# Attention inside a two-layer network: order of projections, f32r transposition of maxima, and who loads and places what

## The chip, the core and the metric

The kernel runs on one core of a Trainium2 chip. The metric is the device time in microseconds of one execution. The core has TensorE (matmul), VectorE, ScalarE, GpSimd and SyncE, which here does nothing but issue DMAs; each works through its own instructions in order, and semaphores tie them together.

## What is computed

The reference is a network of two layers on an x of 2 x 1024 tokens with 256 features. Four branches are added to x one after another:

```
x = x + L0_attn(L0_cond(x))        # causal attention, 16 heads of 16
x = x + L0_ffn(L0_cond2(x))        # mixture of MLPs, then a filter in frequency
x = x + L1_attn(L1_cond(x))        # chosen expert, then a recurrent layer
x = x + L1_ffn(L1_cond2(x))        # layer norm, attention, layer norm, mixture of experts
```

Only the two attentions and the stages just ahead of them matter here. An attention is

```
q, k, v = h @ Wq, h @ Wk, h @ Wv                  # (2, 1024, 16 heads, 16)
scores  = q @ k^T, -inf above the diagonal
out     = softmax(scores / 4) @ v @ Wo (+ bo)
```

## The kernel before

The stages (`prepare`, `attention` "a0", ..., `gated_weight`, `layer_norm`, `attention` "a1", ...) stand one behind another, each a block with one program per engine and a barrier at its end. `first_branches` and `last_branch` call them.

An attention works in eight groups (NG): 2 batches times 4 sets of 4 heads. A group has the following steps.

- `qk`: two projections (one per half h of the 1024 tokens) of queries and keys, in f32 (`qk_projection`, L487). ScalarE rounds each to f32r (`upper`, L602), VectorE subtracts what was rounded off (`lower`, L637); both parts go to the tile `comp`. ScalarE does so for a new group only when the DMAs that read `comp` for the group before have landed.
- SyncE copies rows of `comp` by DMA into the layout that the products need: `place_keys` (L413, 6 DMAs, into `kx`, a ring of three) and `place_queries` (L426, 12 DMAs for each half, into `qx`, a ring of two).
- `v`: two projections of the values (L496), copied by VectorE.
- `first`: 48 f32r products of queries by keys in blocks (L512), used only for the maximum of each row, which VectorE takes (`maximum`, L654). There are three PSUM banks for them. The 17th (MAX0 = 16 are ahead of it) is the first that needs the second half of the queries.
- `max`: the negated row maxima, split into two parts, are transposed by matmul with a negated identity (`maxima`, L520), copied by VectorE and placed by 4 DMAs of SyncE (`place_maxima`, L433) as extra rows of `qx`.
- `scores` (L536): 48 products again, transposed and with the maximum subtracted, in 12 steps (STEPS) of 4 heads; ScalarE takes the exponential (L615), GpSimd cuts the diagonal blocks (L466), `values` (L552) multiplies by v.
- `sums` (L561) and `spread` (L571): reciprocals of the sums, multiplied in by VectorE. After the last group, `out` (L584) is the output projection.

All of it is software-pipelined by hand. `before_turns` lists what comes ahead of the first turn: both projections of group 0, its v, its 48 first-pass products, and among them the projections of group 1. `turn(n)` then interleaves, step by step, the scores and values of group n, the first-pass products of group n + 1 (FIRSTS_AFTER says how many after each of the 48 score products), and one small job after each step (SMALL). A pair (name, 2, h) in SMALL is for group n + 2. The resulting list ORDER is walked by every engine, and each picks its own entries. All small jobs share one PSUM bank, so each waits until the one before has been read. The entries `k_slots` and `q_slots` are SyncE's DMAs: keys and the first half of the queries right after the second projection, the second half at the start of the next turn.

In the opening SyncE loads the weights (L400, four DMAs of 256 KB) with the mask (L402) behind the first; VectorE clears `qx` (L632) and waits for the mask ahead of everything else; ScalarE writes rows of ones into `kx` (L605) after its second `upper`. The constants, among them the identity and the negated identity, are loaded in `prepare` (L98).

The order ahead of the first turn and the small jobs, in the code:

```python
FIRSTS_AFTER = ((1, 1, 0, 2), (2, 1, 1, 1), (1, 0, 2, 1), (0, 3, 0, 0),
                (0, 3, 0, 0), (1, 1, 2, 0), (1, 1, 0, 2), (1, 2, 1, 0),
                (1, 1, 1, 1), (1, 2, 0, 1), (2, 0, 0, 2), (1, 3, 0, 1))
SMALL = (("max", 0, 1), ("sums", -1, 1), ("v", 1, 0), ("spread", -1, 1), ("v", 1, 1), ("max", 1, 0),
         ("qk", 2, 0), ("qk", 2, 1), ("sums", 0, 0), None, None, ("spread", 0, 0))
```

## Time and profile before

| | us |
|---|---|
| median of 3 runs | 2849.01 (2847.25 to 2849.82) |
| profiled execution | 2844.19, its span 2842.5 |
| mean granted clock of TensorE | 0.908 |
| first attention: start, first turn, eighth turn | 36.2, 97.3, 417.5 |
| second attention: start, first turn, eighth turn | 1772.8, 1833.7, 2155.6 |

Times in the trace are from the start of the span. TensorE has two clock levels, 1.2 and 2.4 GHz; the granted clock of a stretch is given as a share of the upper one. The lines of matmuls merge instructions of one form that follow one another; their ends are modelled, and they overlap a little. An f32 product shows as two instructions, an f32r product as one. "SPq" is SyncE's queue of DMA issues: its times are those of the issue, not of the transfer.

### The profile page before, as it was taken

Reading aid. Unit: us, or ns where it says so; the run is one execution under the profiler, and the core shown is the slowest. Engines: PE = TensorE matmul, PEld = TensorE weight load, DVE = VectorE, ACT = ScalarE, POOL = GpSimd, SP = SyncE. Lnnn points to the kernel's source line nnn. Section 1 sums busy time; section 2 is a strip of 40 time slices with the busy share of each in tenths; the row PEclk is TensorE's granted clock in tenths of the full one; section 3 lists DMA queues with packets and bytes.
Section 4 is the critical chain, followed back from the end, with each engine's and each line's share of the span. In section 5 each row is a group of like instructions: output and inputs, shape, how many; then the busy total and the mean of one; then the engine's idle time right before and its main releaser. Section 6 shows DMA issues by size and latency. Waiting matters only on the chain. (4 is left out here: it accounts for less than half of the span.)

```text
span 2842.5 us, 33896 instructions
## 1 busy us (share of the span) xinstructions
PE 2370.3 (83%) x11792; PEld 1605.7 (56%) x11792; DVE 1700.3 (60%) x3614; ACT 845.7 (30%) x1605; POOL 387.5 (14%) x274
## 2 busy tenths in 40 slices
PE   6999997799999775666565656799999679999998
PEld 3565653688887543333333332455655458888786
DVE  3766662444443367999999994566663335555544
ACT  2344452222222234111211112254544222222222
POOL 0011110522220300111000110001010121111110
PEclk9899999899999898888788778799999789999999
DMA  4111110311100110000000000211110021111110
GB/s 136 40 30 41 29 32 1 119 45 44 44 15 0 45 65 8 8 8 8 15 0 15 0 0 7 61 29 42 35 35 9 1 76 38 37 37 37 37 37 30
DMA packets 34114, 92.14 MB, mean 32 GB/s; under 512 B 12088, under 2 KB 13112, under 8 KB 30008
## 3 DMA queue, kind: packets, MB, share of 16 engines
q1 hardware_dynamic: 33984, 90.49, 10.5%
q8 instruction: 72, 1.18, 0.2%
q14 instruction: 58, 0.48, 0.1%
HBM read 62.59 MB, written 2.16 MB: 23 GB/s over the span
## 5 line engine op out<-in xcount | busy, mean ns | idle before, releaser
L654 DVE CUSTOM_DVE_ANT_0 a_junk<-pair,a_mask 128x512 f32<-128x512 f32 (+3 forms) x768 | 391.0, 551 | 219.5 <-PE pair L512 218.6
L615 ACT ACTIVATE a_prob<-pair 128x512 f32<-128x512 f32 (+3 forms) x768 | 326.8, 494 | 383.3 <-PE pair L536 380.4
L512 PE MATMUL pair<-a_kx,a_qx 96*128 96x512 f32 (+3 forms) x768 | 261.3, 397 | 56.4 <-DMA a_qx<-a_comp 44.9
L536 PE MATMUL pair<-a_qx,a_kx 98*128 98x512 f32 (+3 forms) x768 | 272.1, 401 | 5.6 <-ACT a_prob L615 5.4
L906 DVE TENSOR_TENSOR mx_h<-pair,mx_g 128x512 f32<-128x512 f32 x128 | 88.5, 692 | 264.3 <-PE pair L725 253.8
L723 PE MATMUL pair<-mx_x_hi,mx_w_lo 128*128 128x512 f32 x512 | 201.4, 393 | 23.7 <-POOL mx_w_lo L787 21.1
L723 PE MATMUL pair<-m_x_hi,m_w_lo 128*128 128x512 f32 x448 | 178.3, 398 | 49.4 <-POOL m_w_lo L787 47.4
L512 PEld LDWEIGHTS pair<-a_kx,a_qx 96*128 96x128 f32 x768 | 153.4, 209 | 108.6 <-issue 60.2
L1247 PE MATMUL pair<-h_stream,r_w_kz 128*128 128x512 f32 x192 | 103.6, 693 | 118.8 <-DVE r_region L1653 113.3
L724 PE MATMUL pair<-mx_x_hi,mx_w_hi 128*128 128x512 f32 x512 | 200.3, 391 | 0.0
L725 PE MATMUL pair<-mx_x_lo,mx_w_hi 128*128 128x512 f32 x512 | 200.2, 391 | 0.0
L906 DVE TENSOR_TENSOR m_h<-pair,m_g 128x512 f32<-128x512 f32 x96 | 66.4, 691 | 220.4 <-PE pair L725 219.3
L536 PEld LDWEIGHTS pair<-a_qx,a_kx 98*128 98x128 f32 x768 | 143.4, 194 | 87.3 <-ACT a_prob L615 45.1
L859 ACT ACTIVATE mx_g<-pair 128x512 f32<-128x512 f32 x128 | 76.6, 598 | 385.6 <-PE pair L725 385.6
L466 POOL TENSOR_SCALAR_AFFINE_SELECT a_prob<-a_prob 128x512 f32<-128x512 f32 x128 | 81.5, 637 | 778.0 <-ACT a_prob L615 778.0
L724 PE MATMUL pair<-m_x_hi,m_w_hi 128*128 128x512 f32 x448 | 177.3, 396 | 0.0
L725 PE MATMUL pair<-m_x_lo,m_w_hi 128*128 128x512 f32 x448 | 177.0, 395 | 0.0
L552 PE MATMUL pair<-a_prob,a_v 128*32 128x512 f32 (+3 forms) x1536 | 164.3, 500 | 1.3 <-POOL a_prob L466 1.2
L1291 PE MATMUL pair<-r_hq,r_spread 128*128 128x256 f32 x320 | 85.9, 435 | 84.3 <-DVE r_region L1782 71.5
L859 ACT ACTIVATE m_g<-pair 128x512 f32<-128x512 f32 x96 | 57.4, 598 | 294.7 <-PE pair L725 294.7
L1247 PEld LDWEIGHTS pair<-h_stream,r_w_kz 128*128 128x128 f32 x192 | 41.0, 224 | 172.8 <-DVE r_region L1653 116.5
L1667 DVE TENSOR_TENSOR r_region<-r_region 128x1536 f32<-128x1536 f32 (+7 forms) x160 | 130.0, 854 | 2.7
(250 smaller groups left out, 4447.4 us busy)
## 6 DMA issues: line engine op xcount, KB each, us to landing
m_raw<-in_L_cond_experts SPq DMA_DIRECT2D x18, 1024.0 KB, 4.9
a_kx<-a_comp SPq DMA_DIRECT2D x96, 128.0 KB, 2.4
a_qx<-a_comp SPq DMA_DIRECT2D x384, 32.0 KB, 1.9
mx_raw<-in_L_ffn_experts SPq DMA_DIRECT2D x24, 512.0 KB, 5.4
mx_wt<-expert_weights SPq DMA_DIRECT2D x8, 1024.0 KB, 4.7
r_w_ring<-in_r_q_w SPq DMA_DIRECT2D x8, 512.0 KB
m_raw<-in_L_cond_experts SPq DMA_DIRECT2D x6, 512.0 KB, 3.6
x_stream<-in_x SPq DMA_DIRECT2D x1, 2048.0 KB, 10.1
```

Source lines behind the costliest of these rows:

```text
L512: nc.tensor.matmul(first_bank[t % FR][:, 0:c1 - c0], qx[0:PRODUCT, m % 2, a, i * P:(i + 1) * P], kx[0:PRODUCT, m % 3, a // 2, c0:c1], star ...
L536: nc.tensor.matmul(score_bank[t % SR][:, q0:TT], kx[0:ROWS, n % 3, a // 2, j * P:(j + 1) * P], qx[0:ROWS, n % 2, a, h * TT + q0:(h + 1) * ...
L552: last = nc.tensor.matmul(value_bank[r, q0:TT], v_sb[:, n % 2, j, r], prob[:, i % RING, a, q0:TT], start=j == 0, stop=j == 4 * h + 3)
L615: nc.scalar.activation(prob[:, i % RING, a, q0:TT], score_bank[t % SR][:, q0:TT], ACT.Exp, scale=SCALE).then_inc(s["b_exp"], 1)
L654: nc.vector.tensor_tensor_reduce(out=junk[:, t % 2, 0:cols], in0=first_bank[t % FR][:, 0:cols], in1=mask[:, m0:m0 + cols], scale=1.0, scal ...
L723: nc.tensor.matmul(out, w_lo, x_hi, start=first, stop=False)
L724: nc.tensor.matmul(out, w_hi, x_hi, start=False, stop=False)
L725: return nc.tensor.matmul(out, w_hi, x_lo, start=False, stop=last)
L859: nc.scalar.activation(g_sb[:, n % 2, :], c.quad[2 * (n % 2)], func).then_inc(q["act"], 1)
L906: nc.vector.tensor_tensor(h_sb[:, n % 2, :], c.quad[2 * (n % 2) + 1], g_sb[:, n % 2, :], ALU.mult).then_inc(q["prod"], 1)
L1247: last = nc.tensor.matmul(bank, w_kz[:, k, part * DI + m * P:part * DI + (m + 1) * P], seq(c.h, b)[:, k, half(h)], start=k == 0, stop=k == ...
L1667: did(tt(pr[:, i, :, :, :], right[:, 3 * i:3 * i + 2, :].unsqueeze(1).broadcast_to([P, 3, 2, n]), left.rearrange("p (j q) n -> p q j n", j ...
```

## The change

It has five parts.

1. In each turn the two projections of queries and keys stand after steps 3 and 4 (before: 6 and 7), the two of v after 6 and 7 (before: 2 and 4), and `spread` of the group before after step 2 (before: 3). The first-pass products are distributed anew over the steps.
2. In the opening the projections of group 1 come later: after the 25th and the 29th first-pass product (before: after the 6th and the 10th).
3. The transposition of the maxima uses both operands as f32r. The negated identity is no longer loaded: ScalarE computes it from the identity at the end of `prepare`.
4. The first half of group 0's queries is placed by 12 DMAs that ScalarE issues; SyncE doesn't issue them any more. ScalarE's rows of ones come after them.
5. The weights of queries, keys and values are loaded in the stage ahead of each attention (`prepare`, `gated_weight`) into a tile that both stages share. The mask is then the first load of the attention itself.

```diff
@@ prepare
-                for dst, src in ((c.ident, "ident"), (c.neg_ident, "neg_ident"), (c.mean_ones, "mean_ones"),
+                for dst, src in ((c.ident, "ident"), (c.mean_ones, "mean_ones"),
                                  (c.sum_pick, "sum_pick")):
                     sp.dma_start(dst[:, :], A[src]).then_inc(s["tables"], 16)
-                sp.wait_ge(s["tables"], 4 * 16)
+                load_qkv(c, A, "L0_qkv", sp)
+                sp.wait_ge(s["tables"], 3 * 16)
...
+                act.wait_ge(s["tables"], 3 * 16)
+                nc.scalar.activation(c.neg_ident[:, :], c.ident[:, :], ACT.Copy, scale=-1.0).then_inc(s["out_ev"], 1)
@@ orders
-FIRSTS_AFTER = ((1, 1, 0, 2), (2, 1, 1, 1), (1, 0, 2, 1), (0, 3, 0, 0),
-                (0, 3, 0, 0), (1, 1, 2, 0), (1, 1, 0, 2), (1, 2, 1, 0),
-                (1, 1, 1, 1), (1, 2, 0, 1), (2, 0, 0, 2), (1, 3, 0, 1))
+FIRSTS_AFTER = ((2, 0, 0, 2), (2, 0, 1, 1), (2, 2, 0, 1), (1, 0, 2, 1),
+                (1, 0, 3, 0), (1, 0, 3, 0), (2, 0, 2, 0), (1, 2, 0, 1),
+                (2, 1, 0, 2), (2, 0, 1, 0), (1, 1, 2, 0), (1, 2, 0, 0))
-SMALL = (("max", 0, 1), ("sums", -1, 1), ("v", 1, 0), ("spread", -1, 1), ("v", 1, 1), ("max", 1, 0),
-         ("qk", 2, 0), ("qk", 2, 1), ("sums", 0, 0), None, None, ("spread", 0, 0))
+SMALL = (("max", 0, 1), ("sums", -1, 1), ("spread", -1, 1), ("qk", 2, 0), ("qk", 2, 1), ("max", 1, 0),
+         ("v", 1, 0), ("v", 1, 1), ("sums", 0, 0), None, None, ("spread", 0, 0))
@@ before_turns
-    firsts(0, 6)
-    shared("qk", 1, 0)
-    firsts(6, 10)
-    shared("qk", 1, 1)
-    firsts(10, MAX0)
+    firsts(0, MAX0)
...
-    firsts(MAX0 + 6, NF)
+    firsts(MAX0 + 6, MAX0 + 9)
+    for h in range(HALF):
+        order.append(("qk", 1, h))
+        firsts(MAX0 + 9 + 4 * h, MAX0 + 13 + 4 * h)
+        order.extend(finished("qk", 1, h))
+    firsts(MAX0 + 17, NF)
@@ attention
+def load_qkv(c, A, w_qkv, sp):
+    for g in range(GROUPS):
+        sp.dma_start(c.w_qkv[:, g, :, :, :], A[w_qkv][:, g, :, :, :]).then_inc(c.qkv_in, 16)
...
-                for g in range(GROUPS):
-                    sp.dma_start(w[:, g, :, :, :], A[w_qkv][:, g, :, :, :]).then_inc(s["w_one" if g == 0 else "w_rest"], 16)
-                    if g == 0:
-                        sp.dma_start(mask[:, :], A["causal"]).then_inc(s["mask"], 16)
+                sp.dma_start(mask[:, :], A["causal"]).then_inc(s["mask"], 16)
...
                 def place_queries(m, h):
+                    if (m, h) == (0, 0):
+                        return
...
-                        last = nc.tensor.matmul(bank[0:2 * GH, i * P:(i + 1) * P], mx[:, 4 * h + i, :, :].bitcast(F32).rearrange("p a x -> p (a x)"),
+                        last = nc.tensor.matmul(bank[0:2 * GH, i * P:(i + 1) * P], mx[:, 4 * h + i, :, :].rearrange("p a x -> p (a x)"),
                                                 c.neg_ident[:, :], start=True, stop=True)
...
+                def place_first_queries(m, h):
+                    if (m, h) != (0, 0):
+                        return
+                    act.wait_ge(s["zero0"], GH)
+                    act.wait_ge(s["used"], used("qk", 0, 0))
+                    for a in range(GH):
+                        rows = slice(a * HD, a * HD + HD)
+                        for part, low in enumerate((0, 0, 1)):
+                            r0 = part * 32 + a % 2 * HD
+                            act.dma_start(qx[r0:r0 + HD, 0, a, half(0)].bitcast(F32), comp[rows, low, half(0)].bitcast(F32))\
+                                .then_inc(s["q_in0"], 16)
```

## Rows read from the trace of the kernel before

**Rows 1.** The page, busy time of TensorE: us (share of the span) xinstructions.

```profile
PE 2370.3 (83%) x11792; PEld 1605.7 (56%) x11792; DVE 1700.3 (60%) x3614; ACT 845.7 (30%) x1605; POOL 387.5 (14%) x274
```

**Rows 2.** Stretches: from:to, us, busy us of each engine, granted clock, DMA.

```profile
61.70:97.30 35.60, 29.96 (x64) 16.16 (x65) 25.00 (x98) 1.19 (x2) 0.00 (x0) 0.60 0.23 53
139.90:188.50 48.60, 46.17 (x332) 28.94 (x328) 29.78 (x112) 22.50 (x52) 5.09 (x8) 0.93 0.14 33
188.50:234.10 45.60, 43.20 (x333) 27.22 (x329) 29.70 (x112) 22.14 (x52) 5.09 (x8) 1.00 0.16 37
139.90:417.50 277.60, 263.13 (x1965) 166.00 (x1961) 177.10 (x666) 132.48 (x310) 30.56 (x48) 0.97 0.14 34
1876.80:2155.60 278.80, 264.28 (x1964) 166.46 (x1960) 177.28 (x664) 132.82 (x310) 30.57 (x48) 0.96 0.15 34
```

**Rows 3.** Waits, whole span: who waited for whom, us in total, times, longest.

```profile
PE pair L512 <- DMA a_qx<-a_comp: 44.9, 14, 8.2
```

**Rows 4.** Timeline of SyncE's issues at the end of a turn: start, us, instruction.

```profile
177.81 4.48 SPq L413 DMA_DIRECT2D a_kx<-a_comp  x6
182.39 15.08 SPq L426 DMA_DIRECT2D a_qx<-a_comp  x24
```

**Rows 5.** Timeline of TensorE: end of turn 1, then turn 2 from 188.5.

```profile
185.36 0.22 PE L536 MATMUL pair<-a_qx,a_kx 98*128 98x128 f32 x1
185.42 1.13 PE L512 MATMUL pair<-a_kx,a_qx 96*128 96x512 f32 x3
...
191.39 0.30 PE L512 MATMUL pair<-a_kx,a_qx 96*128 96x128 f32 x1 [2.35 <-DMA a_qx<-a_comp]
193.44 1.04 PE L520 MATMUL pair<-neg_ident,a_mx 128*8 128x128 f32 x8
200.00 2.05 PE L496 MATMUL pair<-a_w,h_stream 128*128 128x128 f32 x16
201.81 0.42 PE L536 MATMUL pair<-a_qx,a_kx 98*128 98x128 f32 x2
202.06 0.74 PE L512 MATMUL pair<-a_kx,a_qx 96*128 96x256 f32 x3
203.36 1.06 PE L571 MATMUL pair<-ident,a_o_rcp 128*32 128x128 f32 x32
```

**Rows 6.** The page, DMA issues: engine, count, KB each, us from issue to landing.

```profile
a_qx<-a_comp SPq DMA_DIRECT2D x384, 32.0 KB, 1.9
m_raw<-in_L_cond_experts SPq DMA_DIRECT2D x6, 512.0 KB, 3.6
a_mask<-in_causal SPq DMA_DIRECT2D x2, 512.0 KB, 5.0
```

**Rows 7.** Timeline, first attention's opening up to its first product.

```profile
39.69 0.91 DVE L632 MEMSET a_qx<- 128x1024 f32 x1 [0.16 <-issue]
40.28 3.68 PE L487 MATMUL pair<-h_stream,a_w 128*128 128x512 f32 x4 [5.09 <-DMA a_w<-in_L_qkv]
45.45 1.98 PE L487 MATMUL pair<-h_stream,a_w 128*128 128x512 f32 x4 [1.49 <-DVE a_comp L637]
48.10 0.69 DVE L637 TENSOR_TENSOR a_comp<-pair,a_comp 128x512 fp32r<-128x512 f32 x1 [2.71 <-ACT a_comp L602]
52.73 15.06 SPq L426 DMA_DIRECT2D a_qx<-a_comp  x24
61.71 2.35 PE L512 MATMUL pair<-a_kx,a_qx 96*128 96x128 f32 x6 [8.25 <-DMA a_qx<-a_comp]
```

**Rows 8.** Timeline, the same opening between its first product and turn 0.

```profile
69.90 0.69 DVE L637 TENSOR_TENSOR a_comp<-pair,a_comp 128x512 fp32r<-128x512 f32 x1 [5.25 <-ACT a_comp L602]
75.53 0.69 DVE L637 TENSOR_TENSOR a_comp<-pair,a_comp 128x512 fp32r<-128x512 f32 x1 [3.28 <-ACT a_comp L602]
80.04 7.79 SPq L426 DMA_DIRECT2D a_qx<-a_comp  x12
97.73 0.31 PE L512 MATMUL pair<-a_kx,a_qx 96*128 96x128 f32 x1
```

More of the change, by code:

```diff
@@ L330, with attention @@
 BANK_OF = {e: n for n, e in enumerate(e for e in ORDER if e[0] in SHARED)}
-def attention(c, A, tag, w_qkv, w_out, b_out, dest):
+def load_qkv(c, A, w_qkv, sp):
+    for g in range(GROUPS):
+        sp.dma_start(c.w_qkv[:, g, :, :, :], A[w_qkv][:, g, :, :, :]).then_inc(c.qkv_in, 16)
+def attention(c, A, tag, w_out, b_out, dest):
     nc = c.nc
     s = {n: c.sem(f"{tag}_{n}") for n in (
-        "mask", "w_one", "w_rest", "proj", "hi", "k_in", "q_in0", "q_in1", "m_in0", "m_in1", "used", "vp", "a_mm",
+        "mask", "proj", "hi", "k_in", "q_in0", "q_in1", "m_in0", "m_in1", "used", "vp", "a_mm",
         "a_max", "m_hi", "m_lo", "t_mm", "b_mm", "b_exp", "b_cut", "pv", "o_sum", "o_cp", "o_spread", "zero0", "zero1", "ones", "ow", "om")}
@@ L416, in place_queries @@
                 def place_queries(m, h):
+                    if (m, h) == (0, 0):
+                        return
                     sp.wait_ge(s["used"], used("qk", m, h))
-                    if m < 2 and h == 0:
+                    if m < 2:
                         sp.wait_ge(s[f"zero{m}"], GH)
@@ L481, in qk_projection @@
                     if h == 0 and m == 0:
-                        pe.wait_ge(s["w_one"], 16)
-                    if h == 0 and m == 1:
-                        pe.wait_ge(s["w_rest"], (GROUPS - 1) * 16)
+                        pe.wait_ge(c.qkv_in, GROUPS * 16)
                     bank = take("qk", m, h)
@@ L602, in upper @@
                     nc.scalar.activation(comp[:, 0, half(h)], bank_of("qk", m, h), ACT.Copy).then_inc(s["hi"], 1)
-                    if m == 0 and h:
-                        for x in range(3):
-                            nc.scalar.activation(kx[PRODUCT:ROWS, x, :, :].rearrange("p q t -> p (q t)"),
-                                                 c.ident[PRODUCT:ROWS, 0:1].broadcast_to([2, PAIRS * T]), ACT.Copy, bias=1.0)\
-                                .then_inc(s["ones"], 1)
+                def place_first_queries(m, h):
[9 more added lines that the diff above has]
+                                .then_inc(s["q_in0"], 16)
+                    for x in range(3):
+                        nc.scalar.activation(kx[PRODUCT:ROWS, x, :, :].rearrange("p q t -> p (q t)"),
+                                             c.ident[PRODUCT:ROWS, 0:1].broadcast_to([2, PAIRS * T]), ACT.Copy, bias=1.0)\
+                            .then_inc(s["ones"], 1)
                 def probabilities(n, i, a):
@@ L1830, in _ @@
                 sp.dma_start(bias[:, :], A["L1_cond2_bias"]).then_inc(loaded, 16)
+                load_qkv(c, A, "L1_qkv", sp)
             @block.tensor
@@ L2068, in first_branches @@
         freq_mat = c.sb("freq_mat", [P, KD, D], ctx=ctx)
-        prepare(c, A, freq_mat)
-        attention(c, A, "a0", "L0_qkv", "L0_wo", "zero_bias", c.x)
+        with ExitStack() as w_ctx:
+            c.w_qkv = c.sb("w_qkv_0", [P, GROUPS, 2, KD, P], ctx=w_ctx)
+            c.qkv_in = c.sem("qkv_in_0")
+            prepare(c, A, freq_mat)
+            attention(c, A, "a0", "L0_wo", "zero_bias", c.x)
         two_of_eight(c, A)
@@ L2077, in last_branch @@
         v = c.sb("branch", [P, KD, N], ctx=ctx)
-        gated_weight(c, A, v)
-        layer_norm(c, A, "n1", v, c.h, "L1_ffn_ln1")
-        attention(c, A, "a1", "L1_qkv", "L1_wo", "L1_bo", v)
+        with ExitStack() as w_ctx:
+            c.w_qkv = c.sb("w_qkv_1", [P, GROUPS, 2, KD, P], ctx=w_ctx)
+            c.qkv_in = c.sem("qkv_in_1")
+            gated_weight(c, A, v)
+            layer_norm(c, A, "n1", v, c.h, "L1_ffn_ln1")
+            attention(c, A, "a1", "L1_wo", "L1_bo", v)
         layer_norm(c, A, "n2", v, c.h, "L1_ffn_ln2")
@@ L2134, in _constants @@
     return {
-        "ident": ident, "neg_ident": -ident, "mean_ones": np.full((P, P), 1.0 / D, f), "sum_pick": pick,
+        "ident": ident, "mean_ones": np.full((P, P), 1.0 / D, f), "sum_pick": pick,
         "causal": causal,
```

6 lines of the change are left out of this document (3 added, 3 removed).

## The prediction

> **What bounds the kernel now.** The share of busy time comes first: TensorE works 83% of the span and is the engine that sets the time in most stages [rows 1]. The chain of waits ends in the last mixture of experts, which the change doesn't touch. The stages run one after another with barriers between them, so what the two attention stages lose or gain is lost or gained in full. Those are the stages to read. The table of stretches, cut at each turn's first score matmul, shows a turn of 45.6 us in which TensorE has 43.20 us of work, VectorE 29.7 and ScalarE 22.1 (the third line of [rows 2]): inside a turn TensorE is the bound, and every matmul taken off it counts. Its missing 2.4 us are the second thing to see. The table of waits has TensorE's line 512 (the first-pass products) waiting for a DMA of queries 14 times, 44.9 us in all [rows 3]. Two of these are the openings, 8.25 us in the first attention [rows 7] and as good as the same in the second, since 8.2 is the longest. The other 12 (one in each turn 1 to 6 of both attentions) hold 44.9 - 2 x 8.2 = 28.5 us, 2.4 each. The timeline shows the place: one score matmul after the turn begins, TensorE sits 2.35 us [rows 5]. SyncE's timeline shows the cause: keys and queries of a group are issued from 177.81 on, some 0.63 us apiece, 6 of keys and 12 of queries, so the twelfth leaves at about 190 and lands 1.9 us later [rows 4, 6]. The projection that releases them comes at the sixth and seventh step, too late by those 2.4 us. The third thing is TensorE's clock: the turn that begins at 139.9 has the same work and the same wait as the one at 188.5, but takes 48.6 us at a mean clock of 0.93 [rows 2]. Half speed (1.2 GHz) shows up right behind the wait.
>
> **Part 1, projections moved from steps 6 and 7 to steps 3 and 4.** The matmuls are the same; they trade places with those of v. Place the landing: the projections end some 13 us sooner in the turn, and 18 DMAs take 11.3 + 1.9 = 13.2 us. So the queries are there 10 us before the turn's end instead of 2.4 us behind it: all 12 waits go, **28.5 us**. What is late next? Queued on SyncE behind them are the maxima's four DMAs (2.5 us), which aren't wanted before the next turn. The second half of the queries, issued at the start of a turn, is now wanted sooner, since the seventeenth first-pass product stands in step 3 and not in step 4. In the turn at 188.5, step 3 begins at 201.81, 13.3 us in [rows 5]. Off that go the wait (2.35), the shorter transposition (0.65, below) and v's 1.8 us, and spread's 1.0 comes in: 9.5 us, and the product stands about 0.9 behind that, at 10.4. Twelve issues and a landing are 12 x 0.63 + 1.9 = 9.5 us after the start. It holds by 0.9 us, and it is the narrowest cover of the change. ScalarE's rounding of the projection waits for the same DMAs, but from step 4 on, some 3 us later. VectorE has 12 us of slack in a turn; the new distribution of first-pass products puts three in a row where three banks are to be had. I take 0 for that, with -3 to +8 us over 14 turns as bounds.
>
> **The clock.** Over turns 1 to 6 it is 0.97 of 277.6 us and 0.96 of 278.8 us [rows 2]: 8.3 and 11.2 us of full clock not granted. How much of that the time feels: turn 1 against turn 2 without their waits is (48.6 - 2.38) - (45.6 - 2.35) = 3.0 us for 0.07 x 48.6 = 3.4 us withheld, so 0.88. 19.5 x 0.88 = **17 us**, all of which I expect back, since every low stretch of these turns follows the wait of part 1 and turn 2 had little idle time but the wait and stayed at 1.00. Bounds: 8 (something else lets it fall) to 19.
>
> **Part 2, maxima transposed in f32r.** Now the four products of a group are 8 instructions of 128 columns, 1.04 us, 0.13 each [rows 5]: an f32 product is two instructions. The score and first-pass products, which are f32r, are one each, so there will be 4. The nearest rows for one: an f32r score matmul of 128 columns starts at 185.36 and the next matmul at 185.42, 0.06 us; two at 201.81 take until 202.06, 0.125 each [rows 5]. So a group costs 0.24 to 0.50 and saves 0.5 to 0.8. I take 0.65, the middle. Less than nothing is excluded: the count of instructions halves and none gets longer. Of 32 groups two lie in the openings beside VectorE: 30 x 0.65 = **19.5 us** (15 to 24). The negated identity is made by ScalarE in place of a load: one small activation at the very end of the preparation, 0.2 us on the path once, counted below.
>
> **Part 3, the opening.** Weights are loaded a stage ahead. TensorE's first projection starts at 40.28, after 5.09 us for them [rows 7]; it can now start at 36.4, 0.2 of it the new activation. It takes 1.98 us at full clock instead of 3.68. But VectorE's first subtraction waits for its own memsets, which end at 40.6 (40.8 now), and for the mask, issued at once and landing 3.6 to 5.0 us later [rows 6, 7], at 40.0 to 41.4. So it starts at 41.0, not at 39.2; 0.7 for it, 1.98 for the second projection, 0.67 and 0.69 for its rounding and subtraction (45.45 + 1.98 to 48.10 in the row): 45.0, where the rows have 48.10 + 0.69 = 48.8. Of 5.7 us gained on TensorE's side 3.8 are left.
> The first half of group 0's queries is issued by ScalarE, 12 DMAs from 44.3 beside SyncE's keys, where SyncE issued 6 keys and then 24 queries one after another until 67.8 [rows 7]. No row has a DMA issued by ScalarE. Taking SyncE's 0.63 for it, they land at 44.3 + 7.6 + 1.9 = 53.8, against 61.71, when the first product starts: 7.9 us. Bounds: half that pitch 49.9 (keys land at 51, so 51), double the pitch 61.4. ScalarE's rows of ones move behind its DMAs and aren't wanted until turn 0.
> Then 48 first-pass products. VectorE is their bound, busy 25.0 of 35.6 us [rows 2]; it sat 5.25 and 3.28 us for ScalarE, which waited for the second half of the queries and for a projection [rows 8]. Group 1's projections now stand after the 25th and the 29th product. At half clock, which the opening has (0.60), each holds TensorE 3.4 us; the first is partly hidden by the three banks ahead (2.1 us of idle VectorE), the second must wait for the bank of the first and hides nothing (3.8). From the first product to the end of group 1's last subtraction: 17.7 of work + 6.4 idle = 24.1 us, so 53.8 + 24.1 = 77.9, and not 76.2. The 18 DMAs behind it take 13.5 us till they have landed (76.2, where the subtraction ends, to 80.04 + 7.79 = 87.8, and 1.9 more [rows 6, 8]). Before, turn 0 had not begun by then; now only 15 products, 7 us, are left to cover this. So **a new wait of some 6 us stands in turn 0** and its first product starts at 77.9 + 13.5 = 91.4, against 97.73 [rows 8]: 6.3 us gained. The second attention is the same without the 0.2: together, less 1 us for the clock behind the new wait, **11.8 us**. Bounds: 0 (ScalarE's issues at double the pitch) to 22 (projections at 2.4 GHz, which gives 3 us of products, and the quicker issue).
> Four more loads, 1 MB, on SyncE's queue in the preparation and in the stage before the second attention are queued behind all that those stages wait for: nothing, 0 to 2 us if the loads ahead of them are slowed by sharing.
>
> On that the Trainium skill, DMA: Bandwidth & Descriptors, "Issuing engines are not separate DMA queues", speaks against the change: transfers begun by different engines share the same 16 DMA engines, and a second issuer saves only the time of issuing, "usually small relative to the DMA itself". By it the second queue would be worth about nothing. The rows differ on the size: here 12 issues are 7.6 us and a landing 1.9.
>
> **The sum.** 28.5 + 17 + 19.5 + 11.8 = 76.8 us. The profiled execution took 2844.2 us (span 2842.5); it becomes 2767.4. The median of the runs is 2849.0, 4.8 above it, and becomes **2772**.
>
> **The rivals.** (a) The transfers of the two issuers get in each other's way, or ScalarE issues at 1.2 us: the opening gives 0, for which the page's rule speaks; with the transposition at its low price, 28.5 + 17 + 15 = 60: 2789. (b) More than forecast: the opening's projections run at 2.4 GHz and every bound falls on the good side, 92 us: 2757. (c) The wait only changes its place: the second half of the queries misses its product in step 3 (cover 0.9 us, and one issue in these rows took 1.9 instead of 0.6, which uses it up). At 2 us in 12 turns, with the clock lost again, 41 us are missing: 2813. (d) Slower than before: ScalarE stands at the rounding in step 4 with all exponentials queued behind it until that second half has landed; values, banks and TensorE follow it. It begins to cost when the landing comes more than 13 us after the turn's start and cancels everything from 19.5 us on (6.4 us in each of 12 turns); at 20.5 us: 2861. It would need a pitch of 1.5 us where the rows have 0.63. (e) The change doesn't do what it says, the clock aside: the waits go, but the clock falls as often as before: 2789 too.
>
> **How the numbers follow.** Forecast 0.62, (a) 0.11, (b) 0.10, (c) 0.06, (d) 0.03, (e) 0.08. The range reaches from (b) past (a) and (e): 2755 to 2798. About 0.2% (5.7 us) is what a measurement tells from no change. Faster 0.94: all but (d) and a part of what isn't thought of; within 0.2% 0.03; slower 0.03.
>
> **What would show it.** No wait of line 512 for queries at the start of turns 1 to 6, one of some 6 us in turn 0, turns 1 to 5 of 41 to 43 us at a clock of 1.00; line 520 with half its instructions; the first product at about 17.6 us after each attention's start (36.2 in the first, by the table of times) instead of 25.5. It is wrong if ScalarE's DMAs are seen at 1 us and more, if line 512 waits in step 3, or if turns without a wait stay above 43 us.

## The result and the profile after

The changed kernel takes 2768.63 us (median of 4 runs, 2767.3 to 2769.95) against 2848.13 us of the kernel before (4 runs, 2838.16 to 2849.82). The ratio is 0.9726, 95% interval 0.9703 to 0.9749. The forecast was 2772, range 2755 to 2798. The profiled execution has a span of 2768.2 us, 74.3 less than before, at a mean clock of 0.91.

Stretches of the changed kernel, cut at each turn's first score matmul: turns 1 to 6 of both attentions, turn 2, and turn 0 of both (from:to, us, busy us of TensorE, its weight loads, VectorE, ScalarE, GpSimd, granted clock, DMA share, GB/s).

```profile
137.80:381.80 244.00, 243.56 (x1916) 155.73 (x1912) 176.39 (x665) 132.82 (x310) 30.59 (x48) 1.00 0.16 38
1839.40:2083.30 243.90, 243.47 (x1917) 155.79 (x1913) 176.34 (x665) 132.76 (x310) 30.58 (x48) 1.00 0.16 38
178.90:220.20 41.30, 41.30 (x325) 26.20 (x321) 29.73 (x112) 22.28 (x52) 5.10 (x8) 1.00 0.18 41
90.00:137.80 47.80, 42.24 (x273) 26.15 (x271) 30.03 (x114) 22.29 (x51) 5.10 (x8) 0.86 0.18 41
1787.60:1839.40 51.80, 46.23 (x273) 28.40 (x271) 30.44 (x114) 22.45 (x51) 5.10 (x8) 0.78 0.16 38
```

The first three answer to [rows 2]: turns 1 to 6 took 277.6 and 278.8 us and now take 244.0 and 243.9, the clock is 1.00 instead of 0.97 and 0.96, and TensorE is idle nowhere in turn 2. That is 68.5 of the 74.3 us. The last two are the price in turn 0, below: it took 42.6 and 43.0 us before.

The waits of the first-pass products for queries, which were 44.9 us in 14 times [rows 3]:

```profile
PE pair L519 <- DMA a_qx<-a_comp: 18.1, 4, 5.6
```

Four are left, two ahead of the first product and two in turn 0. The timeline of the first attention's opening (start, us, engine, line, tile, in brackets the idle time before and who ended it):

```profile
39.09 0.33 SPq L409 DMA_DIRECT2D a_mask<-in_causal  x1
39.12 1.95 PE L494 MATMUL pair<-h_stream,w_qkv 128*128 128x512 f32 x4 [1.23 <-PEq L84]
44.33 0.69 DVE L655 TENSOR_TENSOR a_comp<-pair,a_comp 128x512 fp32r<-128x512 f32 x1 [0.82 <-DMA a_mask<-in_causal]
45.07 3.14 PE L494 MATMUL pair<-h_stream,w_qkv 128*128 128x512 f32 x4 [4.00 <-DVE a_comp L655]
48.31 7.64 ACTq L620 DMA_DIRECT2D a_qx<-a_comp  x12
49.59 4.09 SPq L420 DMA_DIRECT2D a_kx<-a_comp  x6
58.48 4.05 PE L519 MATMUL pair<-a_kx,a_qx 96*128 96x128 f32 x10 [2.84 <-DMA a_qx<-a_comp]
...
76.39 3.68 PE L494 MATMUL pair<-h_stream,w_qkv 128*128 128x512 f32 x4 [1.74 <-DVE a_comp L655]
83.31 3.71 SPq L420 DMA_DIRECT2D a_kx<-a_comp  x6
96.15 0.77 PE L519 MATMUL pair<-a_kx,a_qx 96*128 96x128 f32 x2 [5.56 <-DMA a_qx<-a_comp]
```

The stage starts at 39.1 (before: 36.2), so the first product comes 19.4 us behind its start, where it came 25.5 behind it [rows 7]. TensorE starts at once, but its second projection waits 4.0 us for VectorE and the mask and then takes 3.14 us, most of it at half speed (1.95 for the first one). ScalarE issues a DMA in 0.64 us beside SyncE's own. The last two lines are the new wait: group 1's keys leave only at 83.31, and turn 0 stands 5.56 us for its queries.

Measured from the start of the stage to the start of turn 1 (trace of both kernels), the openings went from 103.7 to 98.7 us in the first attention and from 103.9 to 102.2 in the second: 6.7 us gained together. The stage ahead of the first attention took 2.9 us longer; that isn't the change's work, for the runs below put that start between 36.8 and 39.6 us whether they load weights in it or not (39.1 with the new turn order alone). The 2 us that are still missing to 74.3 lie behind the start of the second attention's last turn.

### The profile page after: what moved, and what is told of

Same layout as the page of the kernel before. It is cut to its first block and busy times, and to the rows that moved or that the text cites. A ratio compares the mean times of both kernels' runs of the same rounds, so it can differ in the third digit from the quotient of the medians.

```text
span 2768.2 us, 33642 instructions
## 1 busy us (share of the span) xinstructions
PE 2330.0 (84%) x11664; PEld 1586.4 (57%) x11664; DVE 1702.5 (62%) x3614; ACT 846.8 (31%) x1606; POOL 387.3 (14%) x274
## 3 DMA queue, kind: packets, MB, share of 16 engines
q1 hardware_dynamic: 33072, 89.63, 10.5%
## 5 line engine op out<-in xcount | busy, mean ns | idle before, releaser
L672 DVE CUSTOM_DVE_ANT_0 a_junk<-pair,a_mask 128x512 f32<-128x512 f32 (+3 forms) x768 | 394.3, 551 | 190.5 <-PE pair L519 186.9
L543 PE MATMUL pair<-a_qx,a_kx 98*128 98x512 f32 (+3 forms) x768 | 266.4, 394 | 6.5 <-ACT a_prob L633 6.4
L519 PE MATMUL pair<-a_kx,a_qx 96*128 96x512 f32 (+3 forms) x768 | 248.0, 394 | 21.8 <-DMA a_qx<-a_comp 18.1
L1265 PE MATMUL pair<-h_stream,r_w_kz 128*128 128x512 f32 x192 | 103.7, 694 | 118.7 <-DVE r_region L1671 113.3
## 6 DMA issues: line engine op xcount, KB each, us to landing
x_stream<-in_x SPq DMA_DIRECT2D x1, 2048.0 KB, 10.4
```

The lines of the kernel that those rows point to most:

```text
L519: nc.tensor.matmul(first_bank[t % FR][:, 0:c1 - c0], qx[0:PRODUCT, m % 2, a, i * P:(i + 1) * P], kx[0:PRODUCT, m % 3, a // 2, c0:c1], star ...
L543: nc.tensor.matmul(score_bank[t % SR][:, q0:TT], kx[0:ROWS, n % 3, a // 2, j * P:(j + 1) * P], qx[0:ROWS, n % 2, a, h * TT + q0:(h + 1) * ...
L672: nc.vector.tensor_tensor_reduce(out=junk[:, t % 2, 0:cols], in0=first_bank[t % FR][:, 0:cols], in1=mask[:, m0:m0 + cols], scale=1.0, scal ...
L1265: last = nc.tensor.matmul(bank, w_kz[:, k, part * DI + m * P:part * DI + (m + 1) * P], seq(c.h, b)[:, k, half(h)], start=k == 0, stop=k == ...
```

## The experiments

The kernel before was timed again beside each kernel, and its median came out between 2841 and 2848 us, since the clock in its turns falls out differently from run to run; so both the median and the ratio stand with each. As an estimate from the intervals and the scatter below, differences between two ratios are good to some 0.003 or 8 us, those between two medians of kernels without low clock in the turns to some 4 us. The theory to begin with was the prediction's: four terms that add, TensorE the bound. The rivals are named with each run.

**The f32r transposition, undone.**

```diff
-                        last = nc.tensor.matmul(bank[0:2 * GH, i * P:(i + 1) * P], mx[:, 4 * h + i, :, :].rearrange("p a x -> p (a x)"),
-                                                c.neg_ident[:, :], start=True, stop=True)
+                        last = nc.tensor.matmul(bank[0:2 * GH, i * P:(i + 1) * P], mx[:, 4 * h + i, :, :].bitcast(F32).rearrange("p a x -> p (a x)"),
+                                                c.neg_ident[:, :].bitcast(F32), start=True, stop=True)
```

> The changed kernel with the transposition of the maxima as f32 again. My theory: TensorE bounds a turn, so each of 30 groups in the turns costs what its instructions take longer, 0.97 instead of 0.24 us a group: 30 x 0.73 = 22 us slower than the changed kernel, some 2790; turns of 42.6 instead of 41.1, nothing new waits. Rival: the turn has slack beside the transposition (VectorE's maxima), then under 10 us, and turns of under 41.8.

2786.07 us, ratio 0.9808 (0.9788 to 0.9828): 17.4 us slower than the changed kernel by medians, 23 by ratios. The same turn 2, and turns 1 to 6:

```profile
179.80:222.50 42.70, 42.70 (x335) 26.99 (x329) 29.78 (x112) 22.38 (x52) 5.08 (x8) 1.00 0.17 39
137.40:389.80 252.40, 251.97 (x1964) 160.62 (x1961) 176.78 (x665) 133.43 (x310) 30.46 (x48) 1.00 0.16 37
```

252.4 - 244.0 = 8.4 us in six turns of two transpositions: 0.70 each. TensorE bounds the turn, as the theory has it. VectorE's and ScalarE's work hardly moves. Thirty times 0.70 would be 21 us; in the profiles 3.6 of it are hidden by the clock of the second attention's turn 0, which is 0.89 here (48.2 us) and 0.78 in the changed kernel (51.8 us).

**The old order of a turn, in the changed kernel.**

```diff
-FIRSTS_AFTER = ((2, 0, 0, 2), (2, 0, 1, 1), (2, 2, 0, 1), (1, 0, 2, 1),
+FIRSTS_AFTER = ((1, 1, 0, 2), (2, 1, 1, 1), (1, 0, 2, 1), (0, 3, 0, 0),
...
-SMALL = (("max", 0, 1), ("sums", -1, 1), ("spread", -1, 1), ("qk", 2, 0), ("qk", 2, 1), ("max", 1, 0),
-         ("v", 1, 0), ("v", 1, 1), ("sums", 0, 0), None, None, ("spread", 0, 0))
+SMALL = (("max", 0, 1), ("sums", -1, 1), ("v", 1, 0), ("spread", -1, 1), ("v", 1, 1), ("max", 1, 0),
+         ("qk", 2, 0), ("qk", 2, 1), ("sums", 0, 0), None, None, ("spread", 0, 0))
```

> The changed kernel with the old order of a turn (small jobs and first-pass products as before), everything else as changed. My theory: the waits at the start of turns 1 to 6 come back. The projections' place is the same number of steps ahead of the turn's end as before, so the waits are the old 2.4 us (28.5 us in all), with low clock behind many of them (8 to 17 us), and 0.5 us a turn of worse distribution of first-pass products: 37 to 52 us slower than the changed kernel, 2806 to 2821. Rival: the shorter transposition and the earlier second half of queries had removed the wait anyway: within 10 us of the changed kernel.

2837.69 us, ratio 0.9996 (0.9967 to 1.0026): 69 us slower than the changed kernel, well past the 52 expected at most. Of the gain of the whole change nothing was left. The waits for queries (us, times, longest), then turns 1 to 6:

```profile
PE pair L519 <- DMA a_qx<-a_comp: 45.0, 16, 5.6
```

```profile
138.20:418.30 280.10, 266.62 (x1916) 169.47 (x1912) 177.68 (x664) 134.46 (x310) 30.45 (x48) 0.92 0.14 34
1871.20:2149.50 278.30, 263.91 (x1917) 167.99 (x1913) 177.47 (x665) 134.20 (x310) 30.45 (x48) 0.93 0.14 34
```

Two of the 16 waits stand ahead of the first products and two in turn 0; the 12 in turns 1 to 6 hold 27 us, 1.6 to 3.1 each, so they are of the size they had. What is new is the clock: 0.92 and 0.93, where the kernel before had 0.97 and 0.96 with the same waits [rows 2]. This kernel differs from that one in its turns by nothing but the shorter transposition. That gave a second theory: TensorE stands idle in the wait, and the less it has to do around it, the more readily the clock falls; the parts don't add. (The clock's fall behind the wait was borne out by what follows; that it falls more often was not, see below.)

**Each of the two alone.** The new order of a turn alone (both tables, as in the diff of the change):

> The kernel before with the new order of a turn alone (small jobs and first-pass products). My theory: the 12 waits of 28.5 us go, and with them the low clock behind them (17 us); the new distribution gives 0.3 us a turn or so (4 us); the openings stay: 50 us faster than the kernel before, some 2798, turns 1 to 5 of 42.6. Rival (parts add up to more than their sum only together): 28.5 us or less, because the clock goes on falling without the waits.

2794.57 us against 2845.41, ratio 0.9815 (0.9782 to 0.9848): 50.8 us faster, as expected. Turns 1 to 6, turn 2:

```profile
144.20:396.60 252.40, 251.95 (x1965) 161.02 (x1961) 176.91 (x665) 133.53 (x310) 30.46 (x48) 1.00 0.16 37
186.70:229.30 42.60, 42.59 (x333) 27.18 (x329) 29.76 (x112) 22.47 (x52) 5.08 (x8) 1.00 0.17 39
```

No wait, no low clock, and 42.6 us of TensorE in a turn where [rows 2] has 43.2: the new order gives 0.6 us a turn as well.

The f32r transposition alone:

> The kernel before with the f32r transposition of the maxima alone. The run with the old turn order lost 36 us of clock in turns 1 to 6, where the kernel before lost 17, although its waits were no longer. My theory: the shorter transposition leaves TensorE less to do around the wait, and the clock falls more readily, so that the 22 us saved are mostly given back while the wait is there: 0 to 10 us faster than the kernel before, with more low clock in turns 1 to 6 than its 37.6 us. Rival: the transposition is worth its 22 us in any surroundings, and the old turn order lost its clock to the new order's absence in the opening or to chance: 2822 to 2828.

2845.79 us against 2845.41, ratio 0.9992 (0.9967 to 1.0018): nothing. Two neighbouring turns, then turns 1 to 6 of both attentions:

```profile
193.20:237.30 44.10, 41.90 (x324) 26.27 (x320) 29.61 (x111) 22.37 (x52) 5.08 (x8) 1.00 0.16 38
237.30:288.90 51.60, 48.78 (x324) 31.30 (x320) 29.91 (x112) 22.85 (x52) 5.07 (x8) 0.83 0.14 32
143.70:428.30 284.60, 271.33 (x1917) 173.62 (x1913) 177.89 (x665) 134.52 (x310) 30.44 (x48) 0.90 0.14 33
1885.90:2169.30 283.40, 269.36 (x1917) 171.99 (x1913) 177.66 (x665) 134.69 (x310) 30.45 (x48) 0.91 0.14 33
```

Where the clock stays up, the saving is there: 41.9 us of work, 1.3 less than in [rows 2]. In the next turn with the same instructions the clock is 0.83, and 7 us are gone. Over the six turns it is 0.90 and 0.91. The saved work is given back as low clock.

This profile is one of the slower executions (2859.0 us, the median of ten is 2845.79), so 0.90 and 0.91 are lower than usual. But the loss isn't one of this profile: over the whole execution the mean clock of the ten runs is 0.893 to 0.908, median 0.899, that of the 13 runs of the kernel before beside them 0.903 to 0.909, median 0.908. As an estimate, 0.009 of 2845 us are 25.6 us of full clock not granted, which at the 0.88 of the prediction are 22 us, about what the shorter transposition saves.

**Is it the idle time in the wait?** In the kernel with the f32r transposition alone, the wait was filled with matmuls that serve nothing. They go to the bank that the product behind them overwrites, and the queries land no sooner by them.

```diff
                     if t == 0:
+                        if m >= 2:
+                            for _ in range(5):
+                                nc.tensor.matmul(first_bank[t % FR], w[:, 0, 0, 0, :], c.h[:, 0, time(0, 0, TT)],
+                                                 start=True, stop=True)
                         pe.wait_ge(s["k_in"], (m + 1) * PAIRS * 3 * 16)
```

> The kernel before with the f32r transposition alone, and ahead of each of the 12 waits for queries (turns 1 to 6) five f32 matmuls of 512 columns whose result is overwritten: 2.15 us of useless work for TensorE in a wait of 2.4 us. Nothing waits for less or for longer. My theory: TensorE's idle time in the wait, together with the lighter work around it, lets the clock fall; with the time filled the clock stays at 1.00 in turns 1 to 6, where the same kernel without fillers had 120 us of low clock, and turns are 44 to 44.5 us: the 22 us of the transposition appear, and some 17 us of clock: 2805 to 2815. Rival: the wait isn't the cause (the clock falls by the mix of work in the first steps of a turn, or by chance): low clock stays, and the time is that of the kernel before, 2845, or above it by the fillers.

2831.22 us against 2844.28, ratio 0.9955 (0.9938 to 0.9972). The clock did what the theory says, in all 12 turns; behind the stretches the line of the timeline that has the fillers:

```profile
140.20:413.80 273.60, 273.02 (x1977) 167.76 (x1973) 176.64 (x665) 133.27 (x310) 30.59 (x48) 1.00 0.15 35
1872.00:2145.30 273.30, 272.69 (x1977) 167.77 (x1973) 176.72 (x665) 133.25 (x310) 30.59 (x48) 1.00 0.15 35
```

```profile
186.68 4.46 PE L511 MATMUL pair<-h_stream,a_w 128*128 128x512 f32 x10
```

The time missed its forecast by 16 us, and the last line says why: each f32 matmul is two instructions of 0.43 us, so five of them took 4.3 us and not 2.15, and made every turn 2 us longer than its wait. With two:

> As the run with fillers in the waits, but with two f32 matmuls of 512 columns instead of five. The five took 4.3 us (each is two instructions of 0.43), not 2.15, and so made each of 12 turns 2 us longer than its wait. Two take 1.7 us and fit. My theory (idle TensorE in the wait, with light work around it, lets the clock fall): clock 1.00 in turns 1 to 6, turns of 44.2, the waits still there with some 0.6 us left of each: 12 x 2 = 24 us faster than with five fillers, 2805 to 2810. Rival: filling 1.7 of 2.4 us isn't enough, or five fillers had kept the clock up by being more work than the wait was long: low clock comes back in several turns, 2820 and more.

2812.16 us against 2844.36, ratio 0.9891 (0.9874 to 0.9908), 34 us below the same kernel without fillers by medians, 29 by ratios; forecast 2805 to 2810.

```profile
139.30:399.90 260.60, 258.64 (x1940) 160.59 (x1936) 176.62 (x664) 133.23 (x310) 30.46 (x48) 1.00 0.15 36
1856.30:2119.80 263.50, 258.50 (x1940) 160.58 (x1936) 176.66 (x664) 133.23 (x310) 30.46 (x48) 1.00 0.15 36
```

284.6 and 283.4 us became 260.6 and 263.5 by 24 matmuls that do nothing, though the queries land no sooner; about 10 us of that are the slow execution that was profiled without fillers. Some waits of up to 1.5 us are left, and the clock stays at 1.00 behind them too. That settles where the low clock in the turns comes from, for it goes in two ways, with the wait removed (the new order) and with the wait filled: it is TensorE's idle time at their start. In four kernels that have this wait unfilled (before, the old turn, f32r alone, and the next one) the clock fell in 32 of the 48 turns 1 to 6, each time once, and each time 2.3 to 5.2 us into the turn; the wait ends 2.1 to 3.6 us into it. In turns 1 to 6 of all the others it never fell.

What the f32r transposition adds isn't that it falls more often, as the second theory has it. It fell in 8 and 9 of 12 turns in the two kernels with the f32 transposition and in 7 and 8 of 12 in the two with f32r. It stays low for longer: 5.4 us on average against 12.5 (by the clock of each turn; 37 and 54 us of low clock in sum against 106 and 82). Why it does, whether by the lighter work behind the wait or by something else that the shorter turn changes, no run here shows.

**The opening's parts alone**, that is the change without the turn's new order and without f32r.

> The kernel before with the parts of the opening alone (weights a stage ahead, ScalarE's DMAs, group 1's projections later); a turn's order and the f32 transposition as before. My theory: by the starts of turn 1 in the changed kernel's profile (5.0 and 1.7 us sooner after the stage's start) these parts are worth 7 us together and nothing in the turns: 2838 to 2841, or up to 10 us less if the clock in turn 0 falls out well. Rival: they are worth the 12 us predicted, 2833.

2839.57 us against 2844.28, ratio 0.9972 (0.9954 to 0.9990): 5 to 8 us, as the starts of turn 1 said, less than the 11.8 predicted. Turns 1 to 6 of both attentions:

```profile
138.30:424.00 285.70, 270.60 (x1965) 171.32 (x1961) 177.59 (x665) 133.63 (x310) 30.45 (x48) 0.94 0.14 33
1879.70:2156.60 276.90, 263.75 (x1964) 166.87 (x1960) 177.35 (x664) 133.01 (x310) 30.44 (x48) 0.96 0.14 34
```

The first of them lost 8 us more to the clock than in the kernel before, with the same waits and the same f32 transposition; it is the slowest of the ten executions, and it shows how far one profile can be off. This run and the old turn in the changed kernel differ by the transposition alone, f32 here and f32r there: 2839.57 against 2837.69 us, mean clock 0.905 to 0.911 against 0.890 to 0.903. So beside the wait the transposition is worth nothing with the new opening too, and what brings it out is the turn's order.

Alone, the three parts give 51, 0 and 5 us: 56. Together they give 79.5. The difference is the transposition's gain (17 to 23 us above), which is there only when the wait is gone.

**Group 1's projections at their old place in the opening.**

```diff
-    firsts(0, MAX0)
+    firsts(0, 6)
+    shared("qk", 1, 0)
+    firsts(6, 10)
+    shared("qk", 1, 1)
+    firsts(10, MAX0)
...
-    firsts(MAX0 + 6, MAX0 + 9)
-    for h in range(HALF):
-        order.append(("qk", 1, h))
-        firsts(MAX0 + 9 + 4 * h, MAX0 + 13 + 4 * h)
-        order.extend(finished("qk", 1, h))
-    firsts(MAX0 + 17, NF)
+    firsts(MAX0 + 6, NF)
```

> The changed kernel with group 1's projections in the opening where they were (after the 6th and 10th first-pass product). My theory: moving them later brought the new wait of 5.56 us in turn 0; with the second half of group 0's queries now landed 8 us sooner, their old place no longer costs VectorE its 5 us. Group 1's keys and queries land some 13.5 us behind a subtraction at about 31 us after the stage's start, 45 us, ahead of turn 0 at 51. So no wait in turn 0: 2 x 5.6 = 11 us faster than the changed kernel plus up to 10 us of clock, 2748 to 2758. Rival (the change's idea): at the old place ScalarE waits for the queries and VectorE idles 5 and 3 us as before, which costs what the wait in turn 0 costs: within 3 us of the changed kernel.

2749.13 us (2744.51 to 2750.39), ratio 0.9672 (0.965 to 0.9694): 19.5 us faster than the changed kernel, 15 by ratios. Opening and turn 0 of the first attention, turn 0 of the second, and the timeline around the turn's start:

```profile
56.30:87.00 30.70, 26.97 (x60) 15.01 (x61) 24.80 (x98) 4.19 (x4) 0.00 (x0) 0.61 0.23 53
87.00:129.60 42.60, 42.60 (x273) 26.97 (x271) 30.14 (x114) 22.30 (x51) 5.10 (x8) 0.89 0.15 34
1776.30:1819.20 42.90, 42.90 (x274) 27.15 (x272) 30.17 (x114) 22.30 (x51) 5.10 (x8) 0.88 0.15 34
```

```profile
67.45 3.69 SPq L419 DMA_DIRECT2D a_kx<-a_comp  x6
71.23 7.50 SPq L434 DMA_DIRECT2D a_qx<-a_comp  x12
```

Group 1's keys leave at 67.45 instead of 83.31, its queries by 78.7. Turn 0 starts about when it does in the changed kernel (50.0 us after the stage's start; 50.9 there) and doesn't wait: 42.6 and 42.9 us instead of 47.8 and 51.8. From the first product to turn 0 it takes no longer than there either (30.7 us; 31.5 there). Turn 1 starts 6.1 and 9.8 us sooner after the start of its stage. So this part of the change costs 15 to 20 us.

**SyncE issues the first queries again**, ScalarE no DMA.

> The changed kernel with the first half of group 0's queries issued by SyncE behind the keys, as before; ScalarE issues no DMA. My theory: 12 issues of 0.63 stand in SyncE's queue again, which had started 1.3 us behind ScalarE's: the first product comes 4.7 us later in each attention (58.5 to 63.2 in the first), 9 to 10 us slower in all, 2778. Rival (two issuers share what limits them): SyncE's and ScalarE's DMAs had slowed each other, so less than 3 us.

2775.10 us, ratio 0.9767 (0.9746 to 0.9787): 6.5 us slower than the changed kernel (12 by ratios), 9 expected. SyncE's queue, and the first product (stage start 39.6):

```profile
48.91 3.79 SPq L420 DMA_DIRECT2D a_kx<-a_comp  x6
52.81 11.30 SPq L433 DMA_DIRECT2D a_qx<-a_comp  x18
```

```profile
61.80 2.35 PE L517 MATMUL pair<-a_kx,a_qx 96*128 96x128 f32 x6 [6.51 <-DMA a_qx<-a_comp]
```

22.2 us after the start, 2.8 later than in the changed kernel, where 4.7 were expected; in the second attention it is 22.9, 4.1 later. The twelfth of the 18 issues ends at some 60.3 (52.81 + 12 x 0.63), 20.7 us after the start, where ScalarE's twelfth ends 16.8 us after it; but the product follows 1.5 us behind it here, and 2.5 there, where both engines issue at once. The landings tell why: with SyncE alone each DMA of queries lands 1.9 to 2.0 us after the start of its issue and each of keys 2.3 to 2.4, while with both engines issuing it takes up to 3.6 and 3.7 us and falls back when ScalarE is done. ScalarE's own issuing isn't slowed by it. So the rival with the shared limit holds for the landings, at a price of 1 us, and falls for the issues, which are what the change saves. Of the 1.9 us that are missing to the 4.7 in the first attention this is one, and SyncE's issues, which begin 9.3 us after the start of the stage here and 10.5 in the changed kernel, are the rest.

**Weights loaded in the attention's own stage again.**

```diff
-                load_qkv(c, A, "L0_qkv", sp)
...
-                sp.dma_start(mask[:, :], A["causal"]).then_inc(s["mask"], 16)
+                for g in range(GROUPS):
+                    sp.dma_start(w[:, g, :, :, :], A["L0_qkv" if tag == "a0" else "L1_qkv"][:, g, :, :, :]).then_inc(c.qkv_in if g == 0 else c.qkv_rest, 16)
+                    if g == 0:
+                        sp.dma_start(mask[:, :], A["causal"]).then_inc(s["mask"], 16)
```

> The changed kernel with the weights loaded in the attention's own stage as before (first quarter, mask, other three quarters). My theory: the first projection starts 4.1 us later and runs at half speed; its subtraction comes 3.3 us later than behind the memsets and the mask: 3 to 4 us in each attention, 7 us slower than the changed kernel, 2776. Rival: the memsets and the mask are the bound, so loading ahead was hidden anyway: within 2 us.

2769.51 us, ratio 0.9733 (0.9703 to 0.9763): the changed kernel's time. The first product comes 21.8 us after the start instead of 19.4, and in the first attention turn 1 starts 3.5 us later, as expected. But the second attention's turn 1 starts at 99.5 instead of 102.2, though its first product is later too (21.6 instead of 18.8): its turn 0 has a clock of 0.84 (48.4 us), not 0.78 (51.8). So the 7 us expected aren't in the time, and why the clock of that turn 0 is lower in the changed kernel stays open.

**More work for TensorE in the opening**, on top of the variant with the old opening order.

```diff
+                    if m == 0 and h == 0:
+                        filler(5)
...
+                def filler(count):
+                    for _ in range(count):
+                        nc.tensor.matmul(value_bank, w[:, 0, 0, 0, :], c.h[:, 0, time(0, 0, TT)], start=True, stop=True)
...
+                    if m == 0 and v == 1:
+                        filler(5)
...
+                    if m == 0:
+                        nc.tensor.matmul(value_bank[:, 0:256], qx[0:PRODUCT, 0, a, 0:P], kx[0:PRODUCT, 0, a // 2, 0:256],
+                                         start=True, stop=True)
```

The first `filler(5)` stands behind group 0's first projection, the second behind its v, the last matmul (f32r) behind each of its first-pass products.

> The variant with the old opening order, and in the opening matmuls whose result nobody reads (into a free PSUM bank): five of 512 f32 columns behind group 0's first projection and five behind its v, one f32r of 256 columns behind each of group 0's first-pass products. Nothing else is added. My theory: the opening runs at the lower clock because TensorE has little to do; with fillers it is granted the upper one, group 1's projections hold VectorE 1.5 us less each, and turn 0 has no low clock (10 us of it cost 4): 5 to 7 us in each attention, 10 to 14 us faster than that variant, 2735 to 2740. Rival: at the lower clock product and filler take 0.65 us where VectorE needs 0.5, so the opening gets longer by up to 7 us each and the clock doesn't rise: slower than that variant.

2750.48 us, ratio 0.9664 (0.9633 to 0.9694): the variant's own 2749. Openings from the first product on, then turns 0, of both attentions:

```profile
57.40:87.20 29.80, 26.80 (x110) 19.40 (x110) 24.88 (x98) 4.29 (x4) 0.00 (x0) 0.83 0.24 55
87.20:126.60 39.40, 38.99 (x275) 24.05 (x273) 29.70 (x114) 22.09 (x51) 5.09 (x8) 1.00 0.16 37
1741.80:1774.50 32.70, 30.01 (x110) 23.57 (x110) 25.91 (x99) 5.63 (x5) 0.00 (x0) 0.66 0.23 53
1774.50:1816.80 42.30, 42.30 (x273) 26.65 (x272) 29.68 (x114) 22.31 (x51) 5.09 (x8) 0.90 0.14 32
```

In the first attention it worked (turn 0 at full clock, 3.2 us shorter), in the second it didn't (0.66 and 0.90, and the opening 2 us longer by the fillers). Between these two openings the outcome isn't reliable, and there is no gain on the whole. Inconclusive as to what the opening's clock wants.

**SyncE takes the queries, ScalarE the keys**, on the same variant.

```diff
                 def place_keys(m):
+                    if m == 0:
+                        return
...
                 def place_queries(m, h):
-                    if (m, h) == (0, 0):
-                        return
...
+                place_queries(0, 0)
                 for what, *which in ORDER:
+                    if (what, *which) == ("q_slots", 0, 0):
+                        continue
...
-                    act.wait_ge(s["used"], used("qk", 0, 0))
+                    act.wait_ge(s["used"], used("qk", 0, 1))
+                    for p in range(PAIRS):
+                        rows = slice(64 + p * 32, 96 + p * 32)
+                        for part, low in enumerate((0, 1, 0)):
+                            act.dma_start(kx[part * 32:part * 32 + 32, 0, p, :].bitcast(F32), comp[rows, low, :].bitcast(F32))\
+                                .then_inc(s["k_in"], 16)
```

ScalarE's 12 DMAs of queries are gone from it.

> The variant with the old opening order, where besides SyncE issues the first half of group 0's queries (from the first subtraction on, when it has nothing else to do) and ScalarE the keys, instead of the other way round. My theory: ScalarE can't begin before its second rounding, and its 12 issues of 0.63 end the opening; SyncE begins 4.5 us sooner, and ScalarE's 6 keys end 3.8 us sooner than its 12 queries did. The keys take 0.5 us longer to land: first product 16 us instead of 19 after the stage's start, 2 x 3 = 6 us faster than that variant, 2743. Rival: VectorE and the half clock bound the opening, so the products only start sooner and wait more: under 2 us.

2747.90 us, ratio 0.9660 (0.9628 to 0.9692). The first product comes 17.6 and 16.1 us after the start of the stages (19.3 and 18.9 in the variant), and turn 1 starts 2.7 and 2.9 us sooner. Of these 5.6 us the time shows 1.2, less than it can resolve: the rest of the two profiles differs by nearly as much in the other direction. It is the fastest of the kernels here, and not measurably faster than the variant with the old opening order.

## Why the prediction was right, and where it was not

The time was right to 3.4 us, and the biggest part of it for the reason given. That it is so close is partly luck: two terms missed in opposite directions by 4 to 7 us each, and a rule of the sum was wrong though it did no harm here. Of the 68.5 us of turns 1 to 6, the waits are 28.4, 24 transpositions at 0.70 are 16.8, 12 turns at 0.6 are 7.2, and 16.1 are left for the clock.

- **The waits, 28.5 us.** Right: all 12 are gone, both in the changed kernel and with the new turn order alone. In turn 2 of the changed kernel the last issue of the queries lands at 211.6, 8.6 us ahead of the next turn (forecast 10).
- **The narrowest cover, 0.9 us.** The seventeenth product stands 10.5 us into the turn (forecast 10.4). The landing was put too late: the issues begin 0.9 us ahead of the turn (178.0) and the last one has landed 8.0 us into it (186.9), so the cover is 2.5 us. That wait never came.
- **The clock, 17 us.** Right in place and size: 1.00 in both sets of turns, some 16 us by the sum above, with the wait as its cause, which the order alone and the fillers show.
- **The transposition, 19.5 us.** The step was 0.65 each; it measured 0.70 between the two kernels. By start-to-start times it is 0.25 us a group now (181.16 to 181.41 in turn 2) where it was 0.97; the lower of my two bounds. What the prediction didn't see is that this term isn't one of its own. It was added to the others as "30 x 0.65" and is worth nothing while the wait stands.
- **The distribution of first-pass products, taken as 0.** With the turn's order alone a turn's work went from 43.2 to 42.6 us, some 7 us in 12 turns; the matmuls are the same. From start to start it lies in the first-pass products: turn 2 has 10.4 us of them before and 9.8 with the new order. That they waited for their bank without the view showing it is likely, but no run shows it.
- **The opening, 11.8 us.** Too high. 6.7 us came by the two traces, 5 to 8 by the run with these parts alone. The first product came at 19.4 and 18.8 us, not 17.6, by two terms: "1.98 for the second projection", which ran mostly at half speed (3.14 and 3.64 us), and the landing of 1.9, for the product stands 2.5 us behind ScalarE's last issue. In the first attention the mask came at the late end of its bounds besides. ScalarE's issues were right (12 in 7.64 us), and rival (a) was right in part: the two issuers' transfers do get in each other's way, by 1 us and not by the whole gain. The new wait in turn 0 was forecast at some 6 us and is 5.56; the clock behind it was put at 1 us for both. Turn 0 has a clock of 0.86 and 0.78 (before 0.95 and 0.94) and is 5.2 and 8.8 us longer than before; with the waits taken off and 2 us of saved work added to each, some 7 us of that are the clock's, an estimate from these rows.
- **Group 1's later projections.** The prediction found the wait they bring, but read it as a part of a gain. With the old place the wait isn't there and nothing takes its place: VectorE's idle stretches for which they were moved away, 5.25 and 3.28 us [rows 8], are 3.49 and 1.63 us at the old place once the queries come earlier, and 1.61 and 3.95 at the new place.
- **The rule on issuing engines.** The Trainium skill, DMA: Bandwidth & Descriptors, "Issuing engines are not separate DMA queues", holds in what it says is saved: the issuing time and no more. Against it stands the price of two issuers that the trace shows: while both issue, a landing of queries takes up to 3.6 us instead of 2.0. Its "usually small" doesn't hold for these DMAs, whose 12 issues take 7.6 us and their landing 2.

## What to carry to other kernels

A short wait on the engine that bounds a kernel is to be priced with the clock behind it, and a gain on that engine is to be counted only once the wait beside it is gone: here the order of work alone gave 51 us, the cheaper matmul nothing beside the wait and 17 to 23 us without it. When DMAs are many and small, count their issues on the queue: these copies of 32 KB are on time if their release is (number of issues) x 0.63 us + 2 us ahead of their use, with up to 1.7 us more for a landing while a second engine issues too. Of a change with several parts, take each away once; one part of this one cost 15 to 20 us that the others paid for. And take the clock's part from many executions: one profile of the same kernel can be 10 us off.

## What the hardware showed that I had not expected

- Waits of 1.6 to 2.8 us at the start of a turn are enough for TensorE's clock to fall to 1.2 GHz for a stretch, in 32 of 48 such turns. How long it stays there changed with the transposition beside the wait: 5.4 us on average with the f32 one, 12.5 with the f32r one, which is 0.7 us shorter (two profiles of each).
- Two useless f32 matmuls (1.7 us) in such a wait kept it at 2.4 GHz in 12 turns of 12 and made the kernel 29 to 34 us faster. In the opening the same means worked in one attention and not in the other.
- Two engines that issue DMAs at once hardly slow each other's issues (0.64 and 0.68 us each, 0.63 for SyncE alone), but their transfers land up to 1.7 us later.
- The kernels that have the waits without fillers scatter by 16 to 38 us over ten or more runs (2822.7 to 2861.1 with f32r alone); those without scatter by 3 to 9 over four, and the one with five fillers by 10 over eight.
